# Routed expert tiles: one list load per tile into a ring of sixteen, with GpSimd copying the row numbers to fixed places

## The reference

```python
scores = sigmoid(xf @ router_w.T)                 # 8192 tokens, 64 experts
# best 4 of 8 groups by the sum of their two best biased scores, then the best 8 experts in them
w = scores_of_topk / sum
order = argsort(topk_idx.reshape(-1), stable=True)   # 65,536 pairs (token, expert) sorted by expert
tok = order // 8
g = ragged_dot(xf[tok], gate_w, group_sizes)      # 512 -> 256
u = ragged_dot(xf[tok], up_w, group_sizes)        # 512 -> 256
o = ragged_dot(silu(g) * u, down_w, group_sizes)  # 256 -> 512
routed = zeros.at[tok].add(o * w_of_pair)
```

## Time and profile before

| | before |
|---|---|
| median of 3 runs | 3992.58 us |
| the profiled execution's own time | 3993.73 us |
| its span | 3992.0 us |
| granted TensorE clock, mean of the span | 0.986 |
| PE busy | 3867.9 us (97%) |
| POOL busy | 1916.5 us (48%) |
| DVE / ACT busy | 1654.4 us (41%) / 1444.0 us (36%) |
| tiles (additions issued) / gathers issued | 532 / 536 |
| experts whose weights are loaded | 29 |

### The profile page before, as it was taken

One profiled execution on the slowest core, in us unless ns is written; L12 is line 12 of the kernel. 1 busy time (PEld: TensorE's weight loads), 2 busy tenths in 40 slices (PEclk: granted clock), 3 DMA queues, 4 the chain that ended last, 5 costly groups with the idle time before them and its releaser, 6 DMA issues.

```text
span 3992.0 us, 90448 instructions
## 1 busy us (share of the span) xinstructions
PE 3867.9 (97%) x19160; PEld 3180.6 (80%) x19161; DVE 1654.4 (41%) x3528; ACT 1444.0 (36%) x2807; POOL 1916.5 (48%) x1598
## 2 busy tenths in 40 slices
PE   6999999999999969999999999999999999999997
PEld 5888888888888758888888888888888888888875
DVE  4555555555555623333333333333333333333332
ACT  3222222222222223343343343434343443444443
POOL 1333333333333545555555555555554655555554
PEclk8999999999999979999999999999999999999998
DMA  5112211112211146676676676767677777777775
GB/s 177 43 49 59 60 47 43 43 55 64 53 43 43 33 102 111 113 140 115 111 141 113 125 128 113 137 117 137 118 140 134 120 137 138 122 140 140 141 139 112
DMA packets 372970, 408.94 MB, mean 102 GB/s; under 512 B 192457, under 2 KB 227409, under 8 KB 372881
## 3 DMA queue, kind: packets, MB, share of 16 engines
q0 software_dynamic: 135872, 280.60, 39.4%
q1 hardware_dynamic: 237010, 127.35, 12.5%
HBM read 228.83 MB, written 178.93 MB: 102 GB/s over the span
## 4 chain that ended last, share of the span: by engine, by line
PE 30%; DMA 19%; SPq 8%; issue 6%; POOLq 1%; POOL 0%; ACT 0%; DVE 0%; DVEq 0%; ACTq 0%
PE bank L1156 18%; DMA out_dram<-o_rows,list_s 11%; PE bank L1174 9%; DMA list_g<-slot_list 5%; SPq L1000 5%; PE bank L1147 2%; SPq L1035 2%; DMA raw_d<-in_L_ffn_down_w_dram 2%; PE bank L1165 2%; DMA x_rows<-y_rows,list_g 1%; SPq L1052 1%; POOLq L1000 0%; SPq L1054 0%; DMA list_s<-slot_list 0%; POOL x_rows L1093 0%
## 5 line engine op out<-in xcount | busy, mean ns | idle before, releaser
L1109 POOL DMA_INDIRECT out_dram<-o_rows,list_s x532 | 857.7, 1612 | 623.3 <-issue 313.5
L421 POOL DMA_INDIRECT slot_list<-ent,pos x512 | 498.8, 974 | 858.4 <-PE bank L445 718.4
L1315 DVE TENSOR_TENSOR e_hf<-bank,e_sg 128x256 f32<-128x256 f32 x532 | 225.9, 425 | 1619.1 <-ACT e_sg L1224 1205.5
L1156 PE MATMUL bank<-w_gu_h,x_h 128*128 x2128 | 836.5, 393 | 5.5 <-DVE w_dn_l L30 4.3
L1156 PE MATMUL bank<-w_gu_h,x_l 128*128 x2128 | 834.0, 392 | 0.0
L1156 PE MATMUL bank<-w_gu_l,x_h 128*128 x2128 | 829.3, 390 | 0.0
L1093 POOL DMA_INDIRECT x_rows<-y_rows,list_g x536 | 540.8, 1009 | 558.5 <-issue 317.2
L1224 ACT ACTIVATE e_sg<-bank 128x256 f32<-128x256 f32 x532 | 203.6, 383 | 955.0 <-PE bank L1156 951.0
L1238 ACT ACTIVATE o_rows<-bank,list_s 128x512 f32<-128x512 f32 x532 | 366.8, 690 | 495.1 <-PE bank L1174 417.1
L1156 PEld LDWEIGHTS bank<-w_gu_h,x_h 128*128 128x128 f32 x2128 | 400.4, 188 | 92.9 <-issue 9.3
L1174 PE MATMUL bank<-w_dn_h,e_h_h 128*128 x1064 | 472.2, 444 | 1.6 <-issue 0.5
(11 more groups left out here) (232 smaller groups left out, 5702.6 us busy)
## 6 DMA issues: line engine op xcount, KB each, us to landing
xin<-in_x_dram SPq DMA_DIRECT2D x16, 1024.0 KB, 7.2
y_rows<-yrow SPq DMA_DIRECT2D x64, 256.0 KB, 3.2
stage_d<-in_x_dram SPq DMA_DIRECT2D x16, 1024.0 KB, 7.2
out_dram<-stage_d SPq DMA_DIRECT2D x16, 1024.0 KB, 4.6
raw_gu<-in_L_ffn_gate_w_dram SPq DMA_DIRECT2D x29, 512.0 KB, 4.1
raw_gu<-in_L_ffn_up_w_dram SPq DMA_DIRECT2D x29, 512.0 KB, 6.5
raw_d<-in_L_ffn_down_w_dram SPq DMA_DIRECT2D x29, 512.0 KB, 7.6
list_g<-slot_list SPq DMA_DIRECT2D x536, 1.0 KB
```

The source lines that it names most:

```text
L421: nc.gpsimd.indirect_dma_start(slots, bass.IndirectOffsetOnAxis(ap=pos[v][:, t, k:k + 1], axis=0), ent[v][:, t, k, :], None).then_inc(scat ...
L1109: nc.gpsimd.indirect_dma_start(out, bass.IndirectOffsetOnAxis(ap=ls[u][:, 0:1].bitcast(U32), axis=0), og[u][:], None, compute_op=ALU.add). ...
L1156: last = nc.tensor.matmul(b_gu[u % 2][:], xp[a][:, u % 2, k, :], wgu[b][:, bass.ds(place, 1), k, :].rearrange("p a n -> p (a n)"), start=( ...
L1315: nc.vector.tensor_tensor(hf[:, u % 2, :], b_gu[u % 2][:, H:2 * H], sg[:, u % 2, :], ALU.mult).then_inc(dve_gu, 1)
```

## The change

The two sets of list buffers go. One tensor `lists` with sixteen places takes their part; tile j uses place j & 15. A list is loaded once and stays until the additions of its tile are made. SP's step n becomes: wait until the previous list of the same u has landed, wait for the additions of tile n-16, load the list of n, `weights(n-2)`. SP no longer waits for gathers.

The indirect DMAs still take their row numbers from fixed buffers. So POOL gets two new instructions per tile: `tensor_copy` of the 128 row numbers from the ring to `from_row` before each gather, and to `to_row` before each addition. After each copy POOL waits for a semaphore that this copy raises. ACT's `weigh` takes its scale from the ring directly.

```diff
-            lg = [sb(f"list_g{n}", [P, 2], I32) for n in range(UN)]
-            ls = [sb(f"list_s{n}", [P, 2], I32) for n in range(UN)]
+            LISTS = 16
+            lists = sb("lists", [P, LISTS, 2], I32)
+            from_row = [sb(f"from_row{n}", [P, 1], I32) for n in range(UN)]
+            to_row = [sb(f"to_row{n}", [P, 1], I32) for n in range(UN)]
...
+            def entry(j, f0, f1):
+                at = j & (LISTS - 1)
+                return lists[:, bass.ds(at, 1), f0:f1].rearrange("p a k -> p (a k)")
...
-                def load_list(dst, s, j):
+                def load_list(j, u, g):
+                    known = isinstance(j, int)
+                    if not known or j >= UN:
+                        sp.wait_ge(list_ld[u], 16 * g)
+                    if not known or j >= LISTS:
+                        sp.wait_ge(added[u], 16 * (g - (LISTS // UN - 1)))
+                        sp.nop(nofuse=True)
                     off = field(sp, j, 0, LROWS - P)
-                    sp.dma_start(dst[:], slots[bass.ds(off, P), :]).then_inc(s, 16)
+                    sp.dma_start(entry(j, 0, 2), slots[bass.ds(off, P), :]).then_inc(list_ld[u], 16)
...
                 def step(g, u):
                     n = g * UN + u
...
+                    load_list(n, u, g)
+                    if not isinstance(n, int) or n >= AHEAD:
+                        weights(n - AHEAD)
...
                 def gather(g, u):
-                    pool.wait_ge(lg_ld[u], 16 * (g + 1))
+                    pool.wait_ge(list_ld[u], 16 * (g + 1))
+                    nc.gpsimd.tensor_copy(from_row[u][:], entry(g * UN + u, 0, 1)).then_inc(pool_from, 1)
+                    pool.wait_ge(pool_from, g * UN + u + 1)
                     pool.nop(nofuse=True)
                     nc.gpsimd.indirect_dma_start(xg[u][:], None, y_rows,
-                                                 bass.IndirectOffsetOnAxis(ap=lg[u][:, 0:1].bitcast(U32), axis=0)).then_inc(x_ld[u], 16)
+                                                 bass.IndirectOffsetOnAxis(ap=from_row[u][:].bitcast(U32), axis=0)
+                                                 ).then_inc(x_ld[u], 16)
 
                 def scatter(m, u, gm):
                     pool.wait_ge(act_do, m + 1)
-                    pool.wait_ge(ls_ld[u], 16 * (gm + 1))
+                    nc.gpsimd.tensor_copy(to_row[u][:], entry(m, 0, 1)).then_inc(pool_to, 1)
+                    pool.wait_ge(pool_to, m + 1)
                     with pool.If(field(pool, m, 6, 1) > 0):
...
                     act.wait_ge(pe_do, j + 2)
-                    act.wait_ge(ls_ld[u], 16 * (g + 1))
+                    act.wait_ge(list_ld[u], 16 * (g + 1))
...
-                    nc.scalar.activation(og[u][:], b_o[u % 2][:], ACT.Copy, scale=ls[u][:, 1:2].bitcast(F32)).then_inc(act_do, 1)
+                    nc.scalar.activation(og[u][:], b_o[u % 2][:], ACT.Copy, scale=entry(j, 1, 2).bitcast(F32)).then_inc(act_do, 1)
```

More of the change, by code:

```diff
@@ L976, in build @@
             raw_gu_ld, raw_d_ld = sem("raw_gu_ld"), sem("raw_d_ld")
-            lg_ld = [sem(f"lg_ld{n}") for n in range(UN)]
-            ls_ld = [sem(f"ls_ld{n}") for n in range(UN)]
+            list_ld = [sem(f"list_ld{n}") for n in range(UN)]
+            pool_from, pool_to = sem("pool_from"), sem("pool_to")
             x_ld = [sem(f"x_rows_ld{n}") for n in range(UN)]
@@ L994, in build @@
             assert MAXT % UN == 0 and NTURN > 2
-            LAG_S = 5
-            LEAD = 5
+            AHEAD = 2
             def field(eng, j, f, top_val):
                 return eng.value_load(trow[0:1, bass.ds(j * FLD + f, 1)], min_val=0 if f != 5 else 4, max_val=top_val)
+            def entry(j, f0, f1):
+                at = j & (LISTS - 1)
+                return lists[:, bass.ds(at, 1), f0:f1].rearrange("p a k -> p (a k)")
             class Turn:
@@ L1058, in step @@
                     n = g * UN + u
[L1059 to L1078, removed]
+                    load_list(n, u, g)
+                    if not isinstance(n, int) or n >= AHEAD:
+                        weights(n - AHEAD)
+                weights(0)
+                for n in range(LISTS):
+                    if n == AHEAD:
+                        load_list(n, n % UN, n // UN)
+                    else:
+                        step(n // UN, n % UN)
                 last_turn = field(sp, 0, 5, NTURN - 1)
-                with sp.Fori(3, NTURN + 1) as g:
+                with sp.Fori(LISTS // UN, NTURN + 1) as g:
                     with sp.If(last_turn >= g - 1):
@@ L1083, in _ @@
                             step(g, u)
-                assert LAG_S == UN + 1
-                sp.wait_ge(added[UN - 1], 16 * last_turn)
-                load_list(ls[UN - 1], ls_ld[UN - 1], UN * last_turn + UN - 1)
+                for u in range(UN):
+                    sp.wait_ge(list_ld[u], 16 * last_turn + 32)
+                    sp.nop(nofuse=True)
             @blk.gpsimd
@@ L1108, in scatter @@
                     pool.nop(nofuse=True)
-                    nc.gpsimd.indirect_dma_start(out, bass.IndirectOffsetOnAxis(ap=ls[u][:, 0:1].bitcast(U32), axis=0),
+                    nc.gpsimd.indirect_dma_start(out, bass.IndirectOffsetOnAxis(ap=to_row[u][:].bitcast(U32), axis=0),
                                                  og[u][:], None, compute_op=ALU.add).then_inc(added[u], 16)
```

## The result

The changed kernel takes 4396.23 us in the median of 4 runs (4387.19 to 4403.46); the kernel before takes 3992.93 us in 4 runs. The ratio is 1.1002, with a 95% interval of 1.0985 to 1.1019: 10% slower, as forecast (4384 us, range 4220 to 4610). The profiled execution took 4403.46 us with a span of 4401.8 us. One of the six runs of a later kernel (POOL's copies one tile ahead) took 6975.55 us at a mean granted clock of 0.754, the other five 3992 to 4008 us at 0.984 to 0.988; it is left out of that kernel's median and ratio, and what slowed it stays open.

The account below looks back on a forecast made before the run. The prediction took PE to bound the kernel at 4.69 us per tile, POOL after the change: 1449.1 + 1 + 531 x 5.48 + 15 + 8.1 = 4383 us of span, median 4384 us, range 4220 to 4610.

Parts of the forecast that it names:

- The bound moves to POOL: Stage of tiles: waits on POOL's own copies end overlap twice per tile; POOL needs 5.48 us against PE's 4.69; forecast 80%.
- The pieces of the round: POOL's round per tile: descriptor making 2.62, to the gather 0.80, to the addition 1.60, copies 0.46; sum 5.48 us (5.22 to 5.94).
- To the addition 1.60: POOL, from the wait behind the second copy to the addition's start: field read, branch, no-op and issue, 1.60 us.
- Two copies 0.46: POOL's two 128 x 1 int32 copies per tile with the gap before each: 0.23 us each, 0.46 together (0.20 to 0.92).
- The address arithmetic at nothing: POOL's register work for the ring's place is done while the engine makes descriptors, so it costs nothing.
- Waits of an expert's first tile, 15 us: Additions for an expert's first tile wait for the previous one to land: 0.5 us for each of 29 experts, 15 us.
- The start: First addition at 1449.1 us as profiled before, plus about 1 us as the first gather starts later for its copy.
- The sum: Whole kernel: 1449.1 + 1 + 2909.9 + 15 + 8.1 = 4383 us of span, median 4384 us, 9.8% slower.
- Rival A: PE stays the bound as POOL's overlap survives; early lists make the kernel faster, about 3963 us; chance 7%.
- C: POOL bounds at its bare minimum, copies nearly free, field reads partly ahead: down to 4.9 us per tile, 4075 us; 7%.
- PE's clock: PE keeps a clock of 1.00 despite pauses of about 0.8 us per tile; a falling clock, 5190 us, got 4%.
- What the page would show: Profile after: PE waits for `x_rows` in nearly each tile, 400 us in all; its share falls to about 88%.

## Why the prediction was right, point by point

- **The bound moves to POOL.** Right. The step that carries it, "overlap is thereby gone at two places in each tile", was shown by taking away the waits and leaving the copies, in both kernels.
- **The pieces of the round.** Descriptor making 2.62: measured 1.615 + 1.013 = 2.63. To the gather 0.80: 0.81. To the addition 1.60: 1.58. Two copies 0.46: 0.40, the term that was mis-sized, by 0.03 each. With the means it is 5.42 us against 5.48 forecast. From the rule of the Trainium skill's "GPSIMD Engine Reference", section "Instruction dispatch", I had worked out 0.10 for a copy, an estimate. The trace agrees in that the copy's record starts early, 0.56 us inside the addition's, but its end lies 0.20 behind. So the cost lies between that estimate and mine.
- **The address arithmetic at nothing.** Right; in the rounds of the loop a copy begins at the latest when the engine comes free, but for 2.2 us in all.
- **Waits of an expert's first tile, 15 us.** In the loop the 27 additions whose table field asks for waits began more than 1.58 us behind their copy, by 15.3 us in all: 26 by 0.3 to 0.8 us, and one by 3.9 us, as the addition ahead of it took 8.4 us to land instead of 4.8. Without that one it would have been 11.4, so the 15 is right partly by luck.
- **What was left out.** The mean distance is 5.528 us, 531 x 5.528 = 2935 us. Of it 531 x 5.42 = 2878 is the sum above and 15 are those waits. The other 42 us, from the same timeline: 24 us of longer issues that come back at fixed intervals (last section), 14 us of copies lengthened while VectorE splits new weights, and 4, nearly all of it in the last three rounds, behind the loop. The prediction had none of the three.
- **The start.** 1449.1 + 1 forecast, 1458.5 measured. 8.1 us of this lie ahead of the stage: SP's first list load starts at 1420.6 us before and at 1428.7 after, in a part of the kernel that the change doesn't touch. The profiled executions simply differ there: in a second one of the changed kernel the first addition came at 1446.7 us.
- **The sum.** Errors of opposite sign: the round too long by 0.06 us (-32 us), 42 us left out, and the start 8 us too early. The span came out 19 us above the forecast of 4383, and the median 12 us above 4384. The mechanism is right; that the time is off by 0.3% only is luck, since errors of 32 us one way and some 50 the other partly cancel.
- **Rival A, had it come true.** Its 3963 us left out what new tensors do to TensorE's pace, 21 us, which no step of the prediction held. The version that makes it come true, with copies ahead and the old places, is 0.76% faster than before (forecast 0.74%). Whether the 5 us that I gave the clock are in it was not measured. In the changed kernel itself no two additions are less than 5.28 us apart, so neither A nor C (4.9 us) came true even in part.
- **PE's clock.** Right in what matters: 0.99. In a stretch near the end (4200 to 4300 us) it was 0.95, and TensorE, with 0.7 us of slack in each round, bore it: the undisturbed rounds there still take 5.39 to 5.41 us.
- **What the page would show.** I forecast a PE share of 88% and 400 us of waits for `x_rows`; it is 91% and 178 us for PE, 325 us for its weight loads. The page puts a part of the waiting into busy time.

## What to carry to other kernels

An engine with a low busy share can be one wait away from being the bound: add up one round of its sequencer's and its engine's work, once overlapped and once in a row. A wait on something that the same queue has just issued turns the one sum into the other; issue the producer one round earlier, or give it to an engine that is idle, and the wait is free as long as the round stays below the bound. Two such waits don't cost twice what one does: the first may be hidden in the slack, and the second pays for all.

## What the runs showed of the hardware that I had not expected

TensorE's pace depends on where the tensors of the stage lie: 0.227 us from one 512-column matmul to the next in one place, 0.232 with them 128 bytes further (the change) and 0.234 with them 96 bytes further. The weights stayed where they were, so it is one of the tensors behind the lists: the split rows `x_h` and `x_l`, which TensorE reads as well, or another. Which one, and which boundary, stays open.

The record of a copy behind a descriptor-making instruction is no measure of its cost: 0.76 us behind an addition, 0.20 behind a gather, and both cost 0.20. The Trainium skill's "Perfetto Trace Analysis", section "GPSIMD Engine Instruction", calls the recorded span of a GPSIMD instruction unreliable and advises to time by start-to-start spacing instead; the trace agrees with the first. The 0.20 is taken from the ends, since the copy's start lies inside the addition's record.

Some issues of an indirect DMA take longer, at even intervals. Each 36th addition (14 of them) begins 0.89 us late and each 53rd gather (9 of them) 1.29 us late. In the timeline of POOL after:
```profile
2031.78 0.76 POOL L1094 COPY from_row<-lists 128x1 int32 x1
2034.63 1.00 POOL L1097 DMA_INDIRECT x_rows<-y_rows,from_row  x1 [2.10 <-issue]
...
2046.42 0.20 POOL L1103 COPY to_row<-lists 128x1 int32 x1
2049.09 1.60 POOL L1115 DMA_INDIRECT out_dram<-o_rows,to_row  x1 [2.47 <-issue]
```
The additions' late ones come every 199 us after the change. In the trace of before it is the additions with the same numbers, every 171 us, so it goes by a count and not by time; whether it counts DMAs or turns of the loop, no run tells apart. In the mean, POOL's slack hid it before. What it is stays open.

Beside the work that VectorE does on weights, POOL's takes longer: an addition of 1.60 us took 2.52, a copy of 0.20 took 1.17. All 12 additions over 1.7 us overlap such work of VectorE, and none of the 505 that don't overlap any takes more than 1.62 (timeline after):
```profile
2733.77 2.52 POOL L1115 DMA_INDIRECT out_dram<-o_rows,to_row  x1 [1.59 <-issue]
...
2738.40 1.17 POOL L1103 COPY to_row<-lists 128x1 int32 x1
...
2737.73 2.40 DVE L30 TENSOR_TENSOR w_gu_l<-raw_gu,w_gu_h  x2
```
